# Attention stages whose values are weighed in 4 goes for 12, with narrow key tiles packed in pairs and five probability buffers for three

## The reference

```
x = x + 0.5 * ffn(layernorm(x))     # 8 experts, each token to its best one, hidden width 512
x = x + attention(layernorm(x))     # 16 heads of width 8, rotary positions, causal
x = x + 0.5 * ffn(layernorm(x))
attention: score = q k^T / sqrt(8), masked above the diagonal; softmax; times v; times Wo
```

## Time and profile before

| | us |
|---|---|
| three timed runs | 904.07, 913.01, 908.73 (median 908.73) |
| profiled execution, its own time | 911.38 |
| its span | 909.6 |
| PE busy, DVE busy, ACT busy, POOL busy | 781.4, 615.6, 506.6, 324.6 |
| mean granted clock of TensorE | 0.926 |

### The profile page before, as it was taken

How to read it: one execution, slowest core, us unless ns; L and a number is a source line. 1 busy time by engine, 2 the same in 40 slices (tenths; PEclk the granted TensorE clock), 3 DMA queues, 4 the chain that set the end, 5 groups by cost and what they waited for, 6 DMA issues and landing times. The chain is left out here.

```text
span 909.6 us, 17801 instructions
## 1 busy us (share of the span) xinstructions
PE 781.4 (86%) x5522; PEld 442.6 (49%) x5570; DVE 615.6 (68%) x1919; ACT 506.6 (56%) x1229; POOL 324.6 (36%) x606
## 2 busy tenths in 40 slices
PE   9757889988889999999999999999999876577795
PEld 8657778654323333333333333333333345476785
DVE  5625467569887788778877887788778419344463
ACT  2125456167337676767676767676767751154462
POOL 7253544546522233223322332233223310535543
PEclk8759899999779999999999999999999988689898
DMA  9511111206550332133213321332130010211100
GB/s 304 212 39 29 38 35 35 110 22 167 158 85 6 54 54 36 19 54 55 35 20 54 55 37 19 54 54 36 20 54 2 3 32 38 92 28 37 39 31 27
DMA packets 27990, 51.84 MB, mean 57 GB/s; under 512 B 7553, under 2 KB 19201, under 8 KB 26497
## 3 DMA queue, kind: packets, MB, share of 16 engines
q1 hardware_dynamic: 21296, 41.04, 19.6%
q0 software_dynamic: 4096, 8.69, 3.6%
q10 hardware_dynamic: 2512, 1.06, 0.5%
HBM read 35.40 MB, written 14.97 MB: 55 GB/s over the span
## 5 line engine op out<-in xcount | busy, mean ns | idle before, releaser
L1456 DVE CUSTOM_DVE_ANT_0 cst<-psS,mask_row 128x768 bf16<-128x768 f32 (+7 forms) x512 | 364.3, 756 | 93.1 <-PE psS L1316 90.6
L1420 ACT ACTIVATE prob<-psST 128x512 f32<-128x512 f32 (+3 forms) x750 | 316.8, 496 | 151.9 <-PE psST L1347 113.3
L1316 PE MATMUL psS<-ks,qs 125*128 125x512 bf16 (+3 forms) x768 | 190.6, 337 | 12.6 <-DVE a_rowmax L1456 12.0
L1347 PE MATMUL psST<-qs,ks 128*128 128x512 bf16 (+3 forms) x703 | 178.9, 324 | 5.3 <-issue 0.4
L1361 PE MATMUL a_psO<-prob,vs 128*32 128x512 f32 (+3 forms) x1536 | 164.1, 499 | 15.8 <-ACT prob L1420 14.6
L1540 POOL TENSOR_TENSOR a_gate<-a_zeros 1x1 f32<-1x1 f32 x128 | 23.4, 183 | 330.5 <-ACT prob L1420 330.5
L1316 PEld LDWEIGHTS psS<-ks,qs 125*128 125x128 bf16 x768 | 56.2, 98 | 162.2 <-DVE a_rowmax L1456 60.5
L1347 PEld LDWEIGHTS psST<-qs,ks 128*128 128x128 bf16 x750 | 68.5, 98 | 99.8 <-ACT prob L1420 49.0
L780 POOL DMA_INDIRECT tok<-rows,f_there_number x64 | 61.6, 963 | 102.0 <-DVE f_number L492 42.4
L729 ACT ACTIVATE f_xnT<-f_ps_half,gb 128x128 f32<-128x128 f32 x64 | 29.3, 457 | 114.2 <-PE f_ps_half L657 57.9
L666 PE MATMUL f_ps_wide<-f_xnT,f_w1s 128*128 x312 | 55.9, 307 | 41.4 <-issue 23.9
(11 more groups left out here) (181 smaller groups left out, 952.7 us busy)
## 6 DMA issues: line engine op xcount, KB each, us to landing
qs<-q_split SPq DMA_DIRECT2D x96, 96.0 KB
rows<-tok SPq DMA_DIRECT2D x8, 536.0 KB, 4.8
ks<-k_split SPq DMA_DIRECT2D x32, 128.0 KB
q_split<-p_part SPq DMA_DIRECT2D x24, 128.0 KB, 2.4
k_split<-p_part SPq DMA_DIRECT2D x24, 128.0 KB, 2.4
ks<-k_split SPq DMA_DIRECT2D x16, 192.0 KB
tok<-x_after_first SPq DMA_DIRECT2D x4, 536.0 KB, 5.2
w<-in_Wb SPq DMA_DIRECT2D x1, 2064.0 KB, 7.9
```

Of the source, the lines that this page charges most:

```text
L1316: last = nc.tensor.matmul(ps[:, a * CH + c0:a * CH + c0 + w], lhs, ks[r][0:PR, h * S + c0:h * S + c0 + w], start=True, stop=True)
L1347: nc.tensor.matmul(score_buffer(s, m)[:, 0:w], ks[r][:, h * S + j * P:h * S + (j + 1) * P], qs[r][:, q_col(h, q0):q_col(h, q0) + w], start ...
L1420: nc.scalar.activation(prob[:, u % RING, h, 0:w], score_buffer(s, u * QH + h)[:, 0:w], ACT.Exp, scale=SCALE).then_inc(exp_done, 1)
L1456: last = nc.vector.tensor_tensor_reduce(out=out[:, a * CH:a * CH + width], in0=ps[:, a * CH:a * CH + width], in1=mask_row[:, S - width:], ...
```

## The change

- Units are lists of pieces. In each chunk the 384-wide and the 128-wide key block share one unit of 512 columns: two score matmuls write two parts of one buffer, one exp covers both. A stage has 10 units: 512, 384 + 128, 256 in chunk 0; five of 512, 384 + 128, 256 in chunk 1.
- Weighings go in four groups of units, (0, 1, 2), (3, 4), (5, 6), (7, 8, 9), placed behind the third score of units 4, 6 and 8 and, for the last group, behind the third score of unit 1 of the next stage. Each unit in a group still has its own waits and its own pv_done.
- `prob` has five buffers (PB). The two new ones take the memory of `part` and `an` of the projection, now in one tensor `spare`; ACT waits in stage 0, before unit 3, until the splits in it are stored.
- `plan` credits a whole group's weighing at once; EXTRAS and the copies out move; stage 0 opens with three units and no weighing.
- The mask of a packed unit is two selects, one for each piece.

```
@@ -50,2 +50,3 @@
 RING = 3
+PB = 5
 
@@ -865,8 +866,13 @@
     total, spread, root, corr, offset = (sb(k, [P, NT]) for k in ("total", "spread", "root", "corr", "offset"))
-    an = [sb(f"an{i}", [P, CB, D]) for i in range(2)]
-    anT = [sb(f"anT{i}", [P, CH]) for i in range(2)]
-    n.outT = anT[0]
+    n.outT = sb("anT0", [P, CH])
+    PARTS = 4 * KINDS * CH // 2
+    spare = sb("spare", [P, PARTS + 3 * CH])
+    an = [spare[:, PARTS + i * CH:PARTS + (i + 1) * CH].rearrange("p (j d) -> p j d", j=CB) for i in range(2)]
+    anT = [n.outT, spare[:, PARTS + 2 * CH:]]
+    n.prob_at = [n.prob[:, i, :, :] for i in range(RING)] + [
+        spare[:, i * QH * CH:(i + 1) * QH * CH].rearrange("p (h c) -> p h c", h=QH) for i in range(PB - RING)]
 
     rot, tmp, rest = ([[n.prob[:, m, 2 * i + k, :] for k in range(2)] for i in range(2)] for m in range(3))
-    part = [[sb(f"part{i}{k}", [P, KINDS, CH], BF16) for k in range(2)] for i in range(2)]
+    part = [[spare[:, (2 * i + k) * KINDS * CH // 2:(2 * i + k + 1) * KINDS * CH // 2].bitcast(BF16)
+             .rearrange("p (m t) -> p m t", m=KINDS) for k in range(2)] for i in range(2)]
     psA, psV = n.psST[0], n.psST[1:3]
@@ -1114,10 +1120,18 @@
     for ch in range(NCH):
-        for j in range((ch + 1) * CB):
-            q0 = max(j * P, ch * CH)
-            units.append((ch, j, q0, (ch + 1) * CH - q0))
+        j0 = ch * CB
+        for tiles in [(j,) for j in range(j0 + 1)] + [(j0 + 1, j0 + 3), (j0 + 2,)]:
+            pieces, at = [], 0
+            for j in tiles:
+                q0 = max(j * P, ch * CH)
+                pieces.append((j, q0, (ch + 1) * CH - q0, at))
+                at += (ch + 1) * CH - q0
+            units.append((ch, pieces, at))
     UN = len(units)
     SC = UN * QH
-    diagonal = [u for u, (ch, j, q0, w) in enumerate(units) if j * P == q0]
-    half_start = [0, CB]
-    half_end = [CB, UN]
+    assert UN % PB == 0
+    diagonal = [u for u, (ch, pieces, w) in enumerate(units) if pieces[0][0] * P == pieces[0][1]]
+    half_start = [0, 3]
+    half_end = [3, UN]
+    groups = [(0, 1, 2), (3, 4), (5, 6), (7, 8, 9)]
+    weigh_at = {(4, 2): 0, (6, 2): 1, (8, 2): 2, (1, 2): 3}
 
@@ -1134,3 +1148,4 @@
     WEIGH_COST = 3
-    att_total = sum((QH + WEIGH_COST) * w for _, _, _, w in units)
+    att_total = sum((QH + WEIGH_COST) * w for _, _, w in units)
+    group_cost = [WEIGH_COST * sum(units[u][2] for u in g) for g in groups]
 
@@ -1141,3 +1156,3 @@
         found, tile = [], 0
-        att = sum((QH + WEIGH_COST) * w for _, _, _, w in units[:OPEN]) if first and not whole else 0
+        att = sum(QH * w for _, _, w in units[:OPEN]) if first and not whole else 0
 
@@ -1153,22 +1168,16 @@
         for u in range(UN):
-            if first and not whole and u == OPEN:
-                for v in range(OPEN - LAG, OPEN):
-                    found.append(("weigh", v, 0))
-                    att += WEIGH_COST * units[v][3]
-                    spread()
-            w = units[u][3]
-            for h in range(0 if first and u < OPEN and not whole else QH):
-                found.append(("score", u, h))
-                att += w
-                if h == 0:
-                    if u >= (OPEN + LAG if first and not whole else LAG):
-                        found.append(("weigh", u - LAG, 0))
-                        att += WEIGH_COST * units[u - LAG][3]
-                    elif u < LAG and not first:
-                        found.append(("weigh", u - LAG, 1))
-                        att += WEIGH_COST * units[u - LAG + UN][3]
+            for h in range(QH):
+                if not first or u >= OPEN or whole:
+                    found.append(("score", u, h))
+                    att += units[u][2]
+                if (u, h) in weigh_at:
+                    g = weigh_at[u, h]
+                    before = g == len(groups) - 1
+                    if not before or not first:
+                        found.append(("weigh", g, int(before)))
+                        att += group_cost[g]
                 spread()
-            for at, what, arg, there in EXTRAS:
-                if at == u and (there or not (first if arg == 1 and what == "turn_out" else last)):
-                    found.append((what, arg, 0))
+                for at, what, arg, there in EXTRAS:
+                    if at == (u, h) and (there or not (first if arg == 1 and what == "turn_out" else last)):
+                        found.append((what, arg, 0))
         att = att_total * 2
@@ -1177,3 +1186,3 @@
 
-    OPEN, OPEN_AFTER, OPEN_TILES = CB, 4, 3
+    OPEN, OPEN_AFTER, OPEN_TILES = half_end[0], 4, 3
 
...
@@ -1196,10 +1205,9 @@
 
-    LAG = 2
     AHEAD = tile_total * tile_cost[0]
 
-    EXTRAS = [(1, "turn_max", 1, True), (4, "turn_out", 1, False), (5, "turn_out", 0, True),
-              (7, "turn_max", 0, False)]
+    EXTRAS = [((1, 1), "turn_max", 1, True), ((3, 3), "turn_out", 1, False), ((6, 3), "turn_out", 0, True),
+              ((7, 3), "turn_max", 0, False)]
     before_loop = [(0, "tile", t) for t in range(MT // 2)] + [(0, "turn_max", 0)]
     before_loop += [(0, "tile", t) for t in range(MT // 2, MT)]
-    OPENED = [arg for what, arg, _ in opening() if what == "weigh"]
+    OPENED = diagonal[:2]
     USES = len(uses(False, False))
...
@@ -1266,3 +1276,3 @@
         if s < NST - 1:
-            return psST[m % 3]
+            return psST[(s * SC + m) % 3]
         return (psST + [psS[0][:, CH:], psS[1][:, CH:]])[m % 5]
...
@@ -1346,20 +1356,24 @@
                 pe.wait_ge(exp_done, s * SC + m - 4)
-            nc.tensor.matmul(score_buffer(s, m)[:, 0:w], ks[r][:, h * S + j * P:h * S + (j + 1) * P],
-                             qs[r][:, q_col(h, q0):q_col(h, q0) + w], start=True, stop=True).then_inc(scored, 1)
-
-        def weigh(s, r, u):
-
-            ch, j, q0, w = units[u]
-            pe.wait_ge(exp_done, s * SC + (u + 1) * QH)
-            if u in diagonal:
-                pe.wait_ge(masked, s * len(diagonal) + diagonal.index(u) + 1)
-            if u in half_start:
-                pe.wait_ge(v_ready, s + 1)
-                wait(pe, out_copied, 2 * s + half_start.index(u))
-            c0 = q0 - ch * CH
-            for h in range(QH):
-                last = nc.tensor.matmul(psO[32 * h:32 * h + 32, c0:c0 + w], vs[r][:, j, h, :],
-                                        prob[:, u % RING, h, 0:w], start=(j == 0),
-                                        stop=(u + 1 in half_end))
-            last.then_inc(pv_done, 1)
+            for j, q0, w, at in pieces:
+                last = nc.tensor.matmul(score_buffer(s, m)[:, at:at + w], ks[r][:, h * S + j * P:h * S + (j + 1) * P],
+                                        qs[r][:, q_col(h, q0):q_col(h, q0) + w], start=True, stop=True)
+            last.then_inc(scored, 1)
+
+        def weigh(s, r, g):
+
+            for u in groups[g]:
+                ch, pieces, _ = units[u]
+                pe.wait_ge(exp_done, s * SC + (u + 1) * QH)
+                if u in diagonal:
+                    pe.wait_ge(masked, s * len(diagonal) + diagonal.index(u) + 1)
+                if u in half_start:
+                    pe.wait_ge(v_ready, s + 1)
+                    wait(pe, out_copied, 2 * s + half_start.index(u))
+                for j, q0, w, at in pieces:
+                    c0 = q0 - ch * CH
+                    for h in range(QH):
+                        last = nc.tensor.matmul(psO[32 * h:32 * h + 32, c0:c0 + w], vs[r][:, j, h, :],
+                                                prob[u % PB][:, h, at:at + w], start=(j == 0),
+                                                stop=(u + 1 in half_end))
+                last.then_inc(pv_done, 1)
 
...
@@ -1406,4 +1418,3 @@
         run(stage)
-        weigh(NST - 1, (NST - 1) % RING, UN - 2)
-        weigh(NST - 1, (NST - 1) % RING, UN - 1)
+        weigh(NST - 1, (NST - 1) % RING, len(groups) - 1)
         end = base(NST - 1, False) + len(uses(False, True))
@@ -1415,7 +1426,11 @@
 
-            ch, j, q0, w = units[u]
-            wait(act, pv_done, s * UN + u - 2)
+            _, _, w = units[u]
+            if s == 0 and u == RING:
+                for i in range(2):
+                    for k in range(2):
+                        act.wait_ge(n.split_stored[i][k], 16 * KINDS * NC8 // 2)
+            wait(act, pv_done, s * UN + u - PB + 1)
             for h in range(QH):
                 act.wait_ge(scored, s * SC + u * QH + h + 1)
-                nc.scalar.activation(prob[:, u % RING, h, 0:w], score_buffer(s, u * QH + h)[:, 0:w], ACT.Exp,
+                nc.scalar.activation(prob[u % PB][:, h, 0:w], score_buffer(s, u * QH + h)[:, 0:w], ACT.Exp,
                                      scale=SCALE).then_inc(exp_done, 1)
@@ -1429,5 +1444,5 @@
             for u in range(UN):
-                if u == 1 and not first:
+                if u == 2 and not first:
                     copy_out(s - 1, 1)
-                if u == half_end[0] + 1:
+                if u == half_end[0] + 2:
```

(22 more changed lines are left out.)

## The result

The changed kernel takes 985.38 us (median of 4 runs, 983.27 to 991.17) against 910.87 for the kernel before. The ratio over all runs is 1.084, 95% interval 1.076 to 1.092 (that of the two medians is 1.082). The forecast was 969, range 945 to 998, slower with 0.87. The profiled execution has a span of 984.0 us against 909.6.

A forecast was written before the change was run, and what follows sets the result against it. TensorE was taken to bound the kernel before, with some 2 us of idle a stage. 14 middle stages x 4.2 + 2.5 (stage 0) - 1 (last) = +60 us on 908.7 gives 969, range 945 to 998.

The forecast's parts named there:

- Period and sum: Attention loop: a middle stage goes from 30.31 to 34.5 us, +4.2; with stage 0 and the last, +60 us.
- The middle stage's idle: ScalarE stands 3.67, 3.41, 3.44 and 3.29 us at the four goes of a stage, together 13.8 us.
- the goes: Runs of weighings in which no score is issued: 2.27 us for three units, 1.85 for two, after entry.
- the stretches of tiles: Three tiles in a row behind each go, the third waiting for the first's reduction: 2.07, 1.81, 2.26 and 2.11 us.
- the wait (0.15): Middle stage, turn_max 1: waits 0.15 us because GpSimd does its split only after the masks of units 8 and 9.
- The sum of a stage: ScalarE in a middle stage: work 18.6, idle at the goes 13.8, further waits between them 2.1, together 34.5 us.
- TensorE's busy time: Middle stage: 8 of 12 weighing entries and exits go, saving 1.92 us; TensorE busy well under 28 of 34 us.
- Rival 1: Clock falls to 1.2 GHz in the thin stretch after units 7 to 9: +2 us a stage, 997 us; chance 0.12.
- one of the prediction's own signs against itself: The attention loop's clock was to stay at 1.00; the prediction called itself wrong if it fell there.
- Stage 0 and the last: Attention's end stages: stage 0 +2.5 us (bounds 0 and +4.2), the last -1 (bounds -2 and +1).
- Rival 2: Inside a go each unit or piece still drains TensorE, so no gain: +17 us, 986 us; chance 0.08.
- Rival 3: ScalarE and VectorE catch up between goes, TensorE alone counts: stage 28.4 us, -29, 880 us; chance 0.08.

The follow-up runs named there:

- e1: Changed kernel with one plan edit, at most one tile placed behind each score, goes kept: 944.74 us, 1.040 of the kernel before.
- e3: Kernel before, with tiles held back four times a stage until three are due and placed in a row: 980.23 us, 1.076 of before.
- e4: Changed kernel with VectorE's reduction cut to the last 256 columns of each tile, part of the row maxima left out: 934.76 us (one run).
- e9: Changed kernel's packed units and five buffers, but ten goes and a written-out stage order from corrected stepping: 859.64 us, 0.948 of the kernel before.
- e10: Kernel before, its 12 goes kept, with a written-out stage order from the corrected stepping: 868.88 us, 0.959 of the kernel before.

## Why the prediction was right, point by point

- *Period and sum.* +4.2 us a middle stage was forecast, +4.85 came. Between the 60 us forecast and the 77.6 of the attention lie 9.1 in the middle stages, 3.5 by the clock, 1.2 in stage 0 and 3.4 in the last; the rest of the kernel gave 3.2 back.
- *The middle stage's idle*, the largest: the goes and the stretches of tiles came within 0.02 us each, but ScalarE's idle at the go of units 7 to 9 was 4.09 us for 3.67. The row of turn_max 1 before that go waits 0.26 us for GpSimd's split (539.86); ScalarE ran out of exps 0.70 us behind the start of that go, 1.09 behind that of units 3 and 4, so it had 0.4 us less in hand. The prediction had the wait (0.15) but let it cost nothing further. That the wait is all of the 0.4 is argued, not tested.
- *The sum of a stage* was partly lucky. 18.6 + 13.8 + 2.1 = 34.5 was forecast for ScalarE's work, the four stands behind goes and its further idle; measured are 19.9 + 14.4 + 0.9 = 35.2. ScalarE was busy 1.3 us more (some 0.7 of it, by an estimate, because the last exp before each of six stands lasts 0.60 us and not 0.485) and idle 1.2 us less outside the four stands (turn_out 1, put at 0.6, shows none); the two misses cancel.
- *TensorE's busy time* was to fall by 1.9 us to "well under 28"; it is 28.83 (28.30 in before). The goes did save it, as their 2.29 and 1.85 us show. A likely part of the answer is in the rows: one score alone is recorded as 0.38 us, two as 0.60, so each break in the stream adds some 0.16 us of busy time, and the rows of a stage show 14 breaks for 8. By that estimate it is 1.0 of the 2.4 us between forecast and measurement; the rest stays open.
- *Rival 1, the clock*, came in part, and with it one of the prediction's own signs against itself. Three times in 14 stages the clock fell to its lower level (1.2 GHz), each time for some 3 us. Three windows: the stretch with a fall; within it the time at 0.50; and, one stage later, the thin stretch behind the go of units 7 to 9, where TensorE was as little busy as before the fall (1.33 of 3 us in both) and the clock stayed:

```profile
509.00:514.00 5.00, 4.01 (x14) 1.93 (x15) 2.95 (x9) 3.87 (x10) 3.08 (x10) 0.66 0.76 122
510.50:513.00 2.50, 2.28 (x7) 0.94 (x7) 1.31 (x4) 1.54 (x5) 1.14 (x4) 0.50 0.78 123
543.43:546.43 3.00, 1.33 (x7) 0.56 (x8) 2.84 (x12) 1.42 (x4) 0.74 (x3) 1.00 0.93 145
```

  The distance of the goes before and after it (478.56, 514.95) is 36.39 for 35.16: 1.2 us a fall, not 2, and 3.5 us in all. Each fall followed the thin stretch behind units 7 to 9 that the rival named. In e1, e3 and e4 the clock stays at 1.00 in all middle stages, so the loss does not hang on it. The Trainium skill ("TensorE: Matmul & The Clock Gate", section "A second HAM failure mode: psum-queue depth-cycling") tells of a kernel in which short idles between groups of matmuls, while PSUM buffers are cycled, make the clock go down and up. The trace agrees in three stages of 14; the other 11 had the same idles at 1.00.
- *Stage 0 and the last* were forecast at +2.5 and -1. Stage 0 lost 3.7 up to turn_max 1 of stage 1, within the bounds. The last stage lost 2.4 (6.5 - 4.85 at the distance above, 0.8 behind it), outside its bounds of -2 and +1: without tiles it runs into the split sooner, and turn_max 1 waits for GpSimd's masks of the packed unit and unit 9:

```profile
788.26 0.22 PE L1334 MATMUL psS<-identb,a_maxparts 128*128 128x128 bf16 x1 [1.24 <-POOL a_maxparts L1539]
```

  The wait of turn_max 1 for the split was priced at 0.15 us in middle stages and left out in the last; the step that failed is this term of the sum, 1.24 of the 3.4 us. The second of the packed unit's two selects is at most half of that wait: the two take 1.21 us, one takes 0.62. At the end of the stage the weighing of unit 9 waits 0.78 us for its mask behind the packed unit's (808.97); the largest such wait in before's last stage was 0.31. Where the rest went was not tested.
- *Rival 2* (gaps inside a go) is excluded by the 2.29 and 1.85 us goes. The Trainium skill ("TensorEngine Tiling (Array Packing)", section "Key Properties") says that changing the tiling mode, and not just the tile, drains TensorE; the trace agrees, as all rows of a go have one mode (128*32) and show no gap.
- *Rival 3* (TensorE stays dense) was wrong for this order. Its reasoning comes near in e9 and e10, where the order leaves TensorE no recorded idle and two goes fewer go with 0.62 us less. With six and four goes no order found got there.
- *What bounds before.* The prediction called TensorE the bound with some 2 us of idle. e10 does the same work in 27.78 us, so at least 2.5 us of the 30.31 were waits. Its steps knew that; its first paragraph read the busy row too literally.

## What to carry to other kernels

When an engine works a hand-made order and short rings couple it to others, price a change of order by stepping the rings with measured durations; busy shares don't show it. Merging work to save switches is at risk when the merged block, plus whatever the planner puts behind it, is longer than what the ring holds (here three exps, 1.45 us): four goes of 1.85 and 2.29 us lost to ten single ones even in a good order. A planner that credits a block at once releases everything due behind it in a row: cap what it may place at one point.

## What the runs showed of the hardware

- Three units weighed one behind the other, in four column groups of 32, cost no gap: 2.29 us for 1280 columns where one unit of 512 takes 1.00 and the rows of before give 1.67 ns a column.
- Entering and leaving the weighing costs TensorE 0.24 us by the rows of before (0.10 and 0.14), an estimate from four rows; e10 and e9 would give 0.31 (0.62 for two), if nothing else in them differed.
- TensorE's clock fell from 1.00 to 0.50 in 3 of 14 stages with the same pattern of waits, each time for 1.2 us of loss, and in none of stages 1 to 14 of before, e1, e3 and e4.
